# Target attention on one core: masks of four pairs in one transfer, and the targets of later rounds loaded in two parts

## What is computed

```python
q = (target_item @ W_q).reshape(b, H, HD)            # b=2048, H=4, HD=32
k = (history_sequence @ W_k).reshape(b, S, H, HD)    # S=200
v = (history_sequence @ W_v).reshape(b, S, H, HD)
scores = jnp.einsum('bhd,bshd->bhs', q, k) / SCALE
scores = jnp.where(mask[:, None, :] == 0, NEG, scores)
attn = jax.nn.softmax(scores, axis=-1)
out = jnp.einsum('bhs,bshd->bhd', attn, v).reshape(b, A)
return out @ W_o
```

## Time and profile before

| what | value |
|---|---|
| median of 3 runs | 579.4 us (577.57, 579.4, 581.89) |
| profiled execution | 578.07 us |
| span of its instructions | 576.1 us |
| granted TensorE clock, mean | 0.993 |
| PE / DVE / POOL / ACT busy | 538.1 / 504.2 / 309.2 / 291.3 us |
| mean DMA rate over the span | 380 GB/s |

### The profile page before, as it was taken

One profiled execution on the slowest core, in us unless ns is written; L12 is line 12 of the kernel. 1 busy time (PEld: TensorE's weight loads), 2 busy tenths in 40 slices (PEclk: granted clock), 3 DMA queues, 4 the chain that ended last, 5 costly groups with the idle time before them and its releaser, 6 DMA issues.

```text
span 576.1 us, 41624 instructions
## 1 busy us (share of the span) xinstructions
PE 538.1 (93%) x18604; PEld 437.8 (76%) x18604; DVE 504.2 (88%) x577; ACT 291.3 (51%) x949; POOL 309.2 (54%) x1126
## 2 busy tenths in 40 slices
PE   5597999999999999999999899999999999999996
PEld 4475878778787877877787787878778787877875
DVE  5657899999999899999998999999999999999970
ACT  2053545554555555455555545545554554555453
POOL 6653456465655556565555556556465645646500
PEclk9799999999999999999999999999999999999999
DMA  8967999999999999999999999999999999999950
GB/s 327 416 259 278 354 406 411 402 405 405 412 404 409 405 406 405 405 413 398 410 406 403 385 395 408 406 403 409 405 405 405 409 402 399 410 407 401 402 213 7
DMA packets 47687, 219.04 MB, mean 380 GB/s; under 512 B 5696, under 2 KB 14416, under 8 KB 47648
## 3 DMA queue, kind: packets, MB, share of 16 engines
q1 hardware_dynamic: 46368, 217.35, 94.8%
q0 software_dynamic: 704, 1.05, 0.5%
q10 hardware_dynamic: 576, 0.25, 0.2%
HBM read 217.58 MB, written 1.05 MB: 380 GB/s over the span
## 4 chain that ended last, share of the span: by engine, by line
PE 71%; DVE 17%; DMA 5%; issue 5%; SPq 1%; ACT 0%; DVEq 0%; POOLq 0%; POOL 0%
PE ps_s L251 27%; PE ps_c L281 23%; DVE blocks L475 15%; PE ps_p L264 7%; PE ps_y L291 6%; PE ps_u L239 3%; PE ps_u L298 3%; DMA x_t<-r_target_item 3%; DMA hist<-r_history_sequence 2%; DVE probs_t L496 1%; SPq L153 1%; PE ps_y L306 1%; ACT p_pad L410 0%; DVE inv_sum L491 0%; SPq L144 0%
## 5 line engine op out<-in xcount | busy, mean ns | idle before, releaser
L475 DVE STREAM_TRANSPOSE blocks<-hist 128x768 f32<-128x768 f32 (+2 forms) x320 | 472.1, 1494 | 25.4 <-DMA hist<-r_history_sequence 23.2
L199 POOL COPY u_pad<-u_sb 32x32 f32<-32x32 f32 x1024 | 236.3, 231 | 111.6 <-ACT u_sb L389 53.7
L251 PE MATMUL ps_s<-blocks,u_pad 128*32 128x200 f32 x4096 | 193.7, 335 | 16.5 <-DVE blocks L475 14.4
L281 PE MATMUL ps_c<-hist,p_pad 64*32 64x128 f32 x12800 | 199.8, 271 | 4.0 <-issue 3.1
L281 PEld LDWEIGHTS ps_c<-hist,p_pad 64*32 64x32 f32 x12800 | 181.8, 105 | 19.8 <-issue 17.3
L410 ACT ACTIVATE p_pad<-ps_p,own 128x200 f32<-128x200 f32 x512 | 170.1, 443 | 42.4 <-PE ps_p L264 42.4
L251 PEld LDWEIGHTS ps_s<-blocks,u_pad 128*32 128x32 f32 x4096 | 122.8, 109 | 72.2 <-issue 26.5
L203 POOL TENSOR_SCALAR bias<-mask 128x200 f32<-128x200 int32 x64 | 56.5, 883 | 128.1 <-DMA mask<-r_mask 127.7
L419 ACT COPY ctx_sb<-ps_c 128x128 f32<-128x128 f32 x128 | 27.8, 269 | 88.5 <-PE ps_c L281 88.5
L393 ACT ACTIVATE probs<-neg_score,neg_max 128x200 f32<-128x200 f32 x64 | 29.4, 459 | 81.2 <-DVE neg_max L484 81.1
L264 PE MATMUL ps_p<-probs_t,place_sel 128*64 128x112 f32 x1024 | 63.7, 267 | 0.8 <-DVE probs_t L496 0.5
(11 more groups left out here) (42 smaller groups left out, 93.0 us busy)
## 6 DMA issues: line engine op xcount, KB each, us to landing
hist<-r_history_sequence SPq DMA_DIRECT2D x128, 832.0 KB, 8.6
hist<-r_history_sequence SPq DMA_DIRECT2D x128, 768.0 KB, 5.9
mask<-r_mask SPq DMA_DIRECT2D x64, 100.0 KB, 8.6
out<-out_sb POOLq DMA_DIRECT2D x21, 48.0 KB, 5.3
x_t<-r_target_item SPq DMA_DIRECT2D x1, 976.0 KB, 16.1
w_in<-L_rec_W_k ACTq DMA_DIRECT2D x1, 64.0 KB, 2.0
w_in<-L_rec_W_q SPq DMA_DIRECT2D x1, 64.0 KB, 2.2
w_in<-L_rec_W_v ACTq DMA_DIRECT2D x1, 64.0 KB, 6.7
```

Source lines behind the costliest of these rows:

```text
L199: pool.tensor_copy(to, source[Q * c:Q * c + Q, a]).then_inc(u_pad_ready, 1)
L251: mm = pe.matmul(ps_s[ring][Q * b:Q * b + Q, 0:S].rearrange("p (t j) -> p t j", j=J), u_pad[ring][:, i, b, c, :], blocks[slot][:, :, c, J ...
L281: mm = pe.matmul(ps_c[alpha][at:at + Q, 0:D], p_pad[rows, t + par, i, :], hist[2 * ring + i][rows, t + par, :], start=(t == 0), stop=(t + ...
L475: dve.transpose(blocks[g % BLOCKS][:, t0:t1].rearrange("p t c k -> p (t c k)"), hist[g % SLOTS][:, t0:t1, :].rearrange("p t d -> p (t d)") ...
```

## The change

Three things change, and the computation stays the same.

**Masks.** The mask array is laid out on the host so that a row holds the 800 integers of four users that stand at the same place in four consecutive pairs. One transfer then loads the masks of four pairs (128 rows of 3200 bytes, 400 KB) into one of two buffers. SP issues the first behind the whole history of pair 0, and batch n behind the history of pair 4n-2; the buffer of batch n-2 must have been turned into bias by then, a wait on `bias_ready` 4(n-1). There are 16 mask transfers in place of 64.

**Targets.** Columns 96 to 479 of `x_t` (rounds 1 to 4) come in a transfer of 192 KB right behind the first masks, columns 480 to 2047 (784 KB) behind the history of pair 2.

**Waits.** PE no longer waits for the targets ahead of `warm(4)`. `combine` in the loop waits for the first part (`soon_loaded`), and ACT waits for the second (`late_loaded`) ahead of the copy of round 4's vectors, which orders it ahead of PE's `combine(5)`.

```diff
+    BATCHED = 4
+    SOON = 5 * ROUND
...
-        mask_sb = [sb(f"mask{n}", [P, S], I32) for n in range(RING)]
+        mask_sb = [sb(f"mask{n}", [P, BATCHED, S], I32) for n in range(2)]
...
-            def load_mask(p):
-                wait(sp, bias_ready, p - RING + 1)
-                rows = mask[p * Q:(p + 1) * Q, :]
-                sp.dma_start(mask_sb[p % RING][:, :],
-                             rows.unsqueeze(1).broadcast_to([Q, H, S])).then_inc(mask_loaded[p % RING], 16)
+            def load_mask(n):
+
+                wait(sp, bias_ready, BATCHED * (n - 1))
+                rows = mask[n * Q:(n + 1) * Q, :]
+                sp.dma_start(mask_sb[n % 2][:, :, :].rearrange("p k s -> p (k s)"),
+                             rows.unsqueeze(1).broadcast_to([Q, H, BATCHED * S])).then_inc(mask_loaded[n % 2], 16)
...
-                    if i == 1 and h == 0 and p == 0:
-                        load_mask(0)
-                if p + 1 < NP:
-                    load_mask(p + 1)
-                if p == 1:
-                    sp.dma_start(x_t[:, ROUND:B], target_t[:, ROUND:B]).then_inc(rest_loaded, 16)
+                if p == 0:
+                    load_mask(0)
+                    sp.dma_start(x_t[:, ROUND:SOON], target_t[:, ROUND:SOON]).then_inc(soon_loaded, 16)
+                if p % BATCHED == 2 and p + 2 < NP:
+                    load_mask(p // BATCHED + 1)
+                if p == 2:
+                    sp.dma_start(x_t[:, SOON:B], target_t[:, SOON:B]).then_inc(late_loaded, 16)
...
             def mask_bias(p):
-                pool.wait_ge(mask_loaded[p % RING], 16 * (p // RING + 1))
-                pool.tensor_scalar(bias[p % 2][:, :], mask_sb[p % RING][:, :], 0.0, BIG,
+                n = p // BATCHED
+                pool.wait_ge(mask_loaded[n % 2], 16 * (n // 2 + 1))
+                pool.tensor_scalar(bias[p % 2][:, :], mask_sb[n % 2][:, p % BATCHED, :], 0.0, BIG,
                                    ALU.is_equal, ALU.mult).then_inc(bias_ready, 1)
...
                 if not isinstance(r, int):
+                    pe.wait_ge(soon_loaded, 16)
                     pe.wait_ge(u_copied, r)
...
             scores(0, 0, 0)
             scores(0, 0, 1)
-            pe.wait_ge(rest_loaded, 16)
             warm(WARM[1])
...
                 act.wait_ge(u_done, r + 1)
+                if (r + 1) * ROUND == SOON:
+
+                    act.wait_ge(late_loaded, 16)
...
-            a = a.reshape(-1, 2, 4, 4, 8, 25).transpose(0, 3, 1, 2, 5, 4).reshape(-1, 200)
+            a = a.reshape(-1, 4, 2, 4, 4, 8, 25).transpose(0, 4, 2, 3, 1, 6, 5).reshape(-1, 800)
```

More of the change, by code:

```diff
@@ L92, in target_attention @@
         x_loaded = sem("x_loaded")
-        rest_loaded = sem("rest_loaded")
+        soon_loaded = sem("soon_loaded")
+        late_loaded = sem("late_loaded")
         x_zero = sem("x_zero")
         hist_loaded = [[sem(f"hist_loaded{n}_{h}") for h in range(2)] for n in range(SLOTS)]
-        mask_loaded = [sem(f"mask_loaded{n}") for n in range(RING)]
+        mask_loaded = [sem(f"mask_loaded{n}") for n in range(2)]
         out_stored = sem("out_stored")
```

## The result

The changed kernel takes 581.4 us (median of 20 runs, 579.1 to 587.1) against 579.5 us for the kernel before (20 runs, 577.0 to 582.3). The ratio is 1.0041, 95% interval 1.0024 to 1.0058: slower by 0.4%, where 1.2% faster was forecast. The profiled execution took 582.3 us with a span of 580.3, which is 4.2 us more than the profiled one of before; the medians differ by 1.9 us, so the two profiled executions show the loss larger than it is on the average. A ratio leaves out executions that lie more than 1.5% above the fastest of their kernel, and is not exactly the quotient of the medians shown.

The account below looks back on a forecast made before the run. PE's wait for targets bounds the start; PE's own work plus a PE-DVE loop bounds the steady round, DMA close behind. From 578.07 us, -3.9 - 0.5 + 0.2 - 1.4 = -5.6 gives 572.5 us, range 569.5 to 578.

Parts of the forecast that it names:

- -3.9: Start: without the wait for targets, the first placement comes near 23.3 us against 27.3, a gain of 3.9 us.
- - 0.5: Start: with no long idle stretch PE's clock stays at its upper level, making the first placement 0.5 us shorter.
- one of the prediction's own signs of being wrong: Start: the prediction is wrong if the first placement waits for its probabilities, expected ready at 22.2 us.
- The rival in which W_o isn't delayed: Start: history rows don't delay W_o, scores end at 17.86, gain 5.8 + 0.5 us, total 570.7 us; chance 0.13.
- 1.8 us: Start: 0.75 MB more history passing beside W_o at 419 GB/s delays W_o by 1.8 us; bounds 0 and 1.8.
- First pass of the loop: Code-fetch holes in the loop's first pass; the first now falls in full DMA traffic and may grow, +0.2 us.
- the start's gain is eaten: Start: longer code stalls, a late transpose or a clock drop cost some 3 us; 575.5 to 577 us; chance 0.09.
- the masks in the steady part: Steady part: fewer mask transfers mean fewer sags to 342 GB/s, 0.6 us less DMA load a round, gaining 1.4 us.
- The rule on 512-byte rows: Masks: DMA runs at line rate from 512-byte rows, so longer rows gain 0 and the total is about 574 us.
- Bunching, the slower one: Steady part: late batches cost the next placement 0.55 us and as much again; 580 to 588 us; chance 0.10.
- the queue gets 0.5 us per pair ahead between batches: Steady part, against bunching: three pairs without masks pass between batches, and the DMA queue gains 0.5 us per pair.
- Since DMA is the second limit ... this does not shorten the 25.10 us round: Steady part: less DMA load leaves the 25.10 us round unchanged and removes only some of 1.7 us of disturbances.

Follow-up runs that it names:

- e7: Changed kernel with only its first mask batch moved back between the two halves of pair 0's history; 582.3 us, ratio 1.0018.
- e6: Kernel before, loading only the first three masks and reusing them, so every later mask is left out; 577.1 us, ratio 0.9964.
- e5: Kernel before with 2.4 MB of unread history loaded into the DMA hole at its first code stall; 587.5 us, one execution.
- e1: Kernel before with the targets' part alone: targets in two parts, no wait ahead of the second warm loop, masks single; 576.9 us, ratio 0.9948.
- e14: Kernel before with each single mask loaded as four transfers of 32 partitions, rows of 800 bytes; 601.4 us, ratio 1.0391.
- e17: Same program as e10, run beside e16: four single masks issued together every fourth pair, eight mask buffers; 584.3 us, ratio 1.0098.
- e16: Kernel before with a ring of eight mask buffers in place of three, still one mask at a time; 581.2 us, ratio 1.0038.
- e9: Kernel before with masks in 3200-byte rows, a quarter of a batch (32 partitions) loaded behind each pair; 597.8 us, ratio 1.0343.
- e11: e1 with the late targets behind the history of pair 4 in place of pair 2; 576.8 us, ratio 0.9959.
- e3: Changed kernel with mask batch 1 behind pair 3 (was 2) and late targets behind pair 4 (was 2); 580.5 us, ratio 1.0006.
- e10: Kernel before with four single masks (800-byte rows) issued together every fourth pair, into eight buffers; 585.1 us, ratio 1.0113.
- e15: Kernel before with the masks' part alone, masks of four pairs in one transfer, run beside batches of two; 582.8 us, ratio 1.0038.
- e4: An earlier profiled execution of the same kernel as e5 (kernel before, DMA hole filled with unread history); took 1776 us.

## Why the prediction was wrong

Its sum was -3.9 - 0.5 + 0.2 - 1.4 = -5.6 us. Measured in the profiled executions: -4.8 at the first placement, +3.4 between there and pair 4, +5.4 on the steps to pair 62, and the rest of the +4.2 at the end.

**Start, right in its mechanism, and a little small.** W_o's matmul was forecast near 10.7 and stands at 10.79; scores ending 19.7, measured 19.86; the clock in 17.9 to 23.7 at 1.00. The placement was forecast at 23.3 and came at 22.47: the second warm loop's 16 matmuls took 1.97 us and not 3.5 (0.12 us each, where the prediction had gone by the first loop's 0.22 "at full clock"). No row shows that clock: the trace's record of the granted clock begins only at 14.75 us before and at 17.00 after, where the first loop ends, and a window without a record prints 1.00. The second loop before, at a recorded 0.50 (23.7 to 27.3 us), took 0.23 us a matmul, so the first loop most likely ran at the lower level as well. The last wait is DVE's transposed probabilities (0.71 us), one of the prediction's own signs of being wrong. First context near 28.8, measured 27.85: 5.3 us won where 4.4 were forecast. DMA share above 0.8 between 31 and 36: 1.00. The rival in which W_o isn't delayed fell by that 10.79, and e7 shows the delay answering to what stands beside it. That 1.8 us came out as 1.85 is partly luck: with the first mask as before, W_o's matmul stands at 8.94 to 9.54 in seven executions and at 10.19 in e6, with a batch between the halves at 9.68 to 9.79, and with history there at 10.71 to 11.29.

**"First pass of the loop ... bounds 0 to +1, I take +0.2", mis-sized.** The mechanism was named, in the right direction and at the right place. Its size was 3.55 - 1.27 = +2.3 us, and a cost wasn't in the term at all: the clock is at its 1.2 GHz level behind the stall (34.06 to 37.48 us), worth 0.6 us on 45 context matmuls and 0.8 on the placement, and again behind the hole at 47.78 (51.13 to 54.54), 0.75 on the 37 score matmuls. The other way, the hole of 1.54 us came down to 0.36. The whole term measured +3.4. The upper bound came from the 2.07 us of another hole. e5 would have been the row that was missing: 3.49 in full traffic. The rival "the start's gain is eaten" had this mechanism and a price of 3 us; it was measured at 3.4, and was given 0.09. Its 575.5 to 577 is what the targets' half alone takes (e1, 576.9).

**"the masks in the steady part ... -1.4", wrong in sign.** Three things failed in this step. First, the sag to 342 GB/s was ascribed to the mask's landing. After the change the rate sags where no mask lands (windows after, between two pairs' histories):

```profile
263.00:264.00 1.00, 0.99 (x58) 0.73 (x43) 1.00 (x1) 0.11 (x1) 0.00 (x0) 1.00 1.00 252
263.50:264.00 0.50, 0.49 (x21) 0.23 (x9) 0.50 (x1) 0.11 (x1) 0.00 (x0) 1.00 0.69 139
```

Over the whole microsecond the DMA share is 1.00 at 252 GB/s, so the engines weren't idle: single history packets took up to 0.96 us there, where the usual is 0.25. Why they did, no run shows. Second, the saving in DMA time was taken as 0.6 us a round; by the packets, a mask in 800-byte rows takes 8 x 38 ns = 0.30 us of each engine's time and a quarter of a batch 2 x 127 ns = 0.25, which is 0.05 us a pair and 0.15 a round. Third, even the whole masks' time was worth 2 us (e6). The rule on 512-byte rows, by which the gain would be 0, came nearer to the result than the row that I set against it, though 38 ns for 800 bytes (21 GB/s) and 127 ns for 3200 (25 GB/s) show that such rows aren't quite at full rate.

**"Bunching, the slower one"** was the rival with the right sign. It named the place, DVE's waits at every fourth pair (a sign of being wrong that the prediction gave too; not all of them reach its 1 us), and a price of 0.55 us a batch and as much again. What the steps lost, 5.4 us on 14 batches, is 0.39 us a batch. The sentence set against it, that the queue gets 0.5 us per pair ahead between batches, supposed a DMA with room; e14 shows there is none. e17 against e16 shows that bunching four masks costs 0.6%. That it is all of the changed kernel's loss isn't shown: by the medians batches of two cost as much as four, and eight buffers cost 0.4% with no bunching. This part of the cause stays open.

**"Since DMA is the second limit ... this does not shorten the 25.10 us round"** was right about gains and blind to losses. At parity there is no cover on either side.

## What to carry to other kernels

When a change moves transfers into a stretch where they are absent, look at which code is executed for the first time there: its fetch shares the DMA engines; here a hole of 1.3 us became 3.5, and the clock was at its lower level behind it. Before making transfers fewer and larger in a full queue, ask whether the consumers can stand the bunch; add a little DMA load by an experiment, and if the step grows one for one, nothing hides a bunch. Look at a transfer's outermost dimension: with 8 there, masks landed by 8 engines and cost 3.4 and 3.9% (e9, e14). In this kernel the best version is the targets' half alone, at 0.995.

## What the hardware showed that I had not expected

- A code-fetch stall of PE at one place of one program: 1.27 us with DMA at 25 GB/s from 31 to 36 us, 3.49 us at 418 GB/s. Each has one 16,384-byte packet of the instruction queue, and PE resumes 1.3 us behind its end.
- The granted clock goes to 0.50 behind the stalls of 3.55 and 2.36 us (after), 3.49 (e5), 2.50 (e11) and 1.98 (e3, from 33.38 us on), and stays at 1.00 behind those of 1.27 and 2.07 (before), 2.35 (e10, e16) and 2.64 (e15). In e17, the program of e10, it falls behind 2.62. The length of the stall alone doesn't decide it.
- A transfer of 32 partitions from 8 outer rows lands in 9 records, not 16, and costs 0.3 us a pair at the same bytes.
- Twice in this study a program with float matmuls took three times as long for a whole execution (e4, 1776 us, and one run of e16, 1812 us), with a granted clock of 1.000.
- A ring of eight mask buffers in place of three, with an unchanged queue, was 0.4% slower in one comparison (1.0018 to 1.0058); no cause found, and its profiled execution shows no longer waits for history than before.
